# A transposed neighbour sum that transposes pairs of count bytes as 16-bit words, and back transposes placed inside the sum before it

## The reference

```python
x = _layernorm(x + _L0_gnn_ref(x, ...))   # two graph convolutions
x = _layernorm(x + _L1_gnn_ref(x, ...))   # two segment means and a GRU cell
x = _layernorm(x + _L2_gnn_ref(x, ...))   # MLP over node, summed edge features, graph
x = _layernorm(x + _L3_gnn_ref(x, ...))   # two neighbour-mean layers
```

```python
feat_in = h @ W_in.T + b_in
feat_out = h @ W_out.T + b_out
a_in = _seg_mean(feat_in[src], dst, N)     # over the edges that enter a node
a_out = _seg_mean(feat_out[dst], src, N)   # over the edges that leave a node
h = _gru_cell(jnp.concatenate((a_in, a_out), axis=1), h, ...)
```

## Time and profile before

| | us |
|---|---|
| median of 3 runs | 1025.28 |
| lowest, highest | 1022.96, 1034.95 |
| profiled execution, its time | 1021.54 |
| span of the profiled execution | 1019.8 |
| TensorE busy | 942.5 |
| VectorE busy | 622.6 |
| ScalarE busy | 483.9 |
| GpSimd busy | 60.2 |

### The profile page before, as it was taken

How to read it: one execution, slowest core, us unless ns; L and a number is a source line. 1 busy time by engine, 2 the same in 40 slices (tenths; PEclk the granted TensorE clock), 3 DMA queues, 4 the chain that set the end, 5 groups by cost and what they waited for, 6 DMA issues and landing times.

```text
span 1019.8 us, 19249 instructions
## 1 busy us (share of the span) xinstructions
PE 942.5 (92%) x7324; PEld 827.3 (81%) x7324; DVE 622.6 (61%) x949; ACT 483.9 (47%) x785; POOL 60.2 (6%) x133
## 2 busy tenths in 40 slices
PE   7599999999689999989989989989999799999995
PEld 6499999999689979989988878845444499969995
DVE  3799999899364455665554445535465655504654
ACT  0245444444565565677547757722532432233233
POOL 1200000000000000000002324400000000000000
PEclk9989999899799999989999989999999899999998
DMA  9767877777100000000000000000000000000001
GB/s 283 142 143 171 178 164 168 155 170 155 30 1 0 0 1 1 1 16 1 0 1 0 0 1 0 0 2 1 11 1 0 22 1 0 0 1 1 1 12 53
DMA packets 168790, 48.11 MB, mean 47 GB/s; under 512 B 155068, under 2 KB 167388, under 8 KB 168713
## 3 DMA queue, kind: packets, MB, share of 16 engines
q1 hardware_dynamic: 155582, 44.96, 19.0%
q10 hardware_dynamic: 12012, 0.83, 0.8%
q0 software_dynamic: 1120, 1.29, 0.5%
HBM read 45.44 MB, written 8.02 MB: 52 GB/s over the span
## 4 chain that ended last, share of the span: by engine, by line
PE 85%; DVE 5%; SPq 3%; ACT 3%; DMA 2%; issue 2%; DVEq 0%; ACTq 0%
PE bank L1638 17%; PE bank L1639 17%; PE bank L1581 10%; PE bank L1571 7%; PE bank L1757 5%; PE bank L1750 4%; PE bank L1758 4%; PE bank L1842 2%; PE bank L1792 2%; PE bank L1543 2%; PE bank L1831 1%; PE bank L1793 1%; PE bank L1686 1%; PE bank L1850 1%; PE bank L1830 1%
## 5 line engine op out<-in xcount | busy, mean ns | idle before, releaser
L1638 PE MATMUL bank<-stage,f_hi 125*128 125x392 f32 x1000 | 347.8, 348 | 8.9 <-DVE f_lo L1096 2.8
L1639 PE MATMUL bank<-stage,f_lo 125*128 125x392 f32 x1000 | 343.5, 343 | 0.0
L1075 DVE CAST stage<-counts 125x2352 fp32r<-125x2352 uint8 (+1 forms) x120 | 165.4, 1380 | 87.4 <-PE bank L1639 87.3
L1638 PEld LDWEIGHTS bank<-stage,f_hi 125*128 125x128 f32 x1000 | 190.7, 191 | 11.4 <-issue 5.6
L1639 PEld LDWEIGHTS bank<-stage,f_lo 125*128 125x128 f32 x1000 | 190.5, 190 | 0.6
L740 ACT ACTIVATE stage<-counts 125x1568 fp32r<-125x1568 uint8 (+1 forms) x80 | 107.8, 1347 | 173.4 <-PE bank L1639 170.7
L1581 PE MATMUL bank<-tmp,wb 128*65 128x25 f32 x2000 | 133.6, 221 | 0.9 <-DMA wb<-in_edge_attr 0.6
L1581 PEld LDWEIGHTS bank<-tmp,wb 128*65 128x65 f32 x2000 | 130.5, 145 | 1.3 <-DMA wb<-in_edge_attr 0.7
L686 ACT ACTIVATE counts<-bank 125x500 uint8<-125x500 f32 x188 | 87.9, 537 | 46.1 <-PE bank L1571 45.2
L844 ACT ACTIVATE stage<-bank 125x500 fp32r<-125x500 bf16 x150 | 87.5, 588 | 36.7 <-PE bank L1750 26.7
L1571 PE MATMUL bank<-rowb,xT 128*128 128x125 bf16 x1250 | 89.8, 229 | 8.4 <-DVE rowb L1007 3.8
(11 more groups left out here) (215 smaller groups left out, 944.9 us busy)
## 6 DMA issues: line engine op xcount, KB each, us to landing
wb<-in_edge_attr SPq DMA_DIRECT2D x125, 256.0 KB, 3.6
lists_d<-in_dst SPq DMA_DIRECT2D x1, 3104.0 KB
lists_d<-in_src SPq DMA_DIRECT2D x1, 3104.0 KB
wa<-in_x SPq DMA_DIRECT2D x25, 62.5 KB
out<-wl SPq DMA_DIRECT2D x6, 250.0 KB
xT<-in_dst SPq DMA_DIRECT2D x63, 4.0 KB, 3.1
xT<-in_dst ACTq DMA_DIRECT2D x62, 4.0 KB, 2.8
wb<-in_L_gnn_w_ih SPq DMA_DIRECT2D x1, 384.0 KB, 3.1
```

What stands on the lines that cost most here:

```text
L1075: nc.vector.tensor_copy(set_buffer(u, m), counts[:, SETS[u][0]:sum(SETS[u]), chunk(pair * 2 + off)]).then_inc(s["set_d_ready"], 1)
L1638: mm(bank[h][:, 0:CH], f_hi[:, first + k, :], rhs[:, k, :], start=(first + k == 0), stop=False)
L1639: last = mm(bank[h][:, 0:CH], f_lo[:, first + k, :], rhs[:, k, :], start=False, stop=(first + k == HI - 1))
```

## The change

The transposed sum is written anew.

- A pair of neighbouring count bytes is read as one 16-bit word (FP16) without conversion. TensorE transposes 128 words x 125 source nodes at a time against a new identity `ident_h`; the result in PSUM has, on partition p, the two counts of target nodes 2p and 2p+1 of a block of 256. The copy from PSUM reads the bytes (stride 2) and writes two tiles of fp32r, one for the even and one for the odd nodes. There are 12 blocks of 128 words and a last one of 32 words, which becomes a single tile of 64 rows. 120 is the new largest count for which the dense path is taken.
- The stationary tiles have to be the features of nodes a, a+2, a+4, ...; they are made anew, in seven sets, by transposing strided columns of `xT` on TensorE (bank 3), with an upper part by ScalarE and a rest by VectorE. `f_cur` and GpSimd's copies are gone.
- Step u transposes the words of step u+1 (eight tiles, then the remaining four or five), and multiplies two tiles per group. ScalarE copies the first eight transposed tiles, VectorE the others. There are no hardware loops.
- Factor rows are spread in the even steps of the first half, and copied by ScalarE; VectorE marks edges in the odd steps, and makes `has_edges` in two parts in the second half. The sums are kept bank by bank, and the waits of the second half and of the gates are by bank.
- The first norm's back transposes are issued inside the third sum, group c-1 in chunk c, ahead of its fourth set; the third sum is unrolled on TensorE and ScalarE.
- `n_small` moves to free columns of `wl1`.

The diff, cut to its core:

```diff
-        f_hi = sb("f_hi", [LO, HI, D], F32R)
-        f_lo = sb("f_lo", [LO, HI, D], F32R)
-        stage = sb("stage", [LO, 2 * NP], F32R)
+        f_hi_all = sb("f_hi", [D, HI, D], F32R)
+        f_lo_all = sb("f_lo", [D, HI, D], F32R)
+        stage_all = sb("stage", [D, 4 * TQ], F32R)
+        ident_h = sb("ident_h", [128, 128], FP16)
...
+        words = counts[:, :, :].bitcast(FP16)
+        def t_words(u, hi):
+            a = u % TT * TW
+            if u % TT < TT - 1:
+                return [(slice(0, TW), words[:, hi, a:a + TW])]
+            return [(slice(0, NP // 2 - a), words[:, hi, a:NP // 2])]
+        def t_pair(u, p):
+            return (THALF[u // TT][0] + 8 * p, (8, 4 + u // TT)[p])
+        def t_bank(u, p):
+            return bank[4 + 2 * (u % 2) + p]
...
# ScalarE
-            rest_of_sum(2, ((0, 0, 1), (0, 0, 3)))
-            for k in (0, 2, 4, 6):
-                keep_back(0, k)
+            for c in range(NC):
+                if c:
+                    widen_set(2, c // 2, c % 2, 1)
+                    widen_set(2, c // 2, c % 2, 3)
+                if c % 2:
+                    keep_back(0, c - 1)
+            def bytes_to_rows(u):
+                act.wait_ge(s["tile_t"], 2 * u + 1)
+                for to, of in t_copies(u, 0):
+                    last = nc.scalar.activation(to, of, ACT.Copy)
+                last.then_inc(s["tile_ev_a"], 1)
+            def source_tiles(j):
+                act.wait_ge(s["f_t"], j + 1)
+                for rows, tiles, made in f_parts(j):
+                    last = nc.scalar.activation(f_hi_all[rows, tiles, :], made, ACT.Copy)
+                last.then_inc(s["f_split"], 1)
+            bytes_to_rows(0)
+            source_tiles(0)
+            for u in range(2 * TT - 1):
+                if u < TT:
+                    if u % 2:
+                        source_tiles(u // 2 + 1)
+                    else:
+                        g, n = GROUPS[u // 2]
+                        act.wait_ge(s["row_made"], NGR + u // 2 + 1)
+                        nc.scalar.activation(wb[:, g * LO:(g + n) * LO], bank[3][:, 0:n * LO], ACT.Copy).then_inc(s["row_kept"], 1)
+                bytes_to_rows(u + 1)
...
# VectorE
+            def keep_sums(half):
+                for k in ((0, 1, 2), (3, 4, 5, 6))[half]:
+                    g, n = GROUPS[k]
+                    dve.wait_ge(s["rows_used"], k + 1)
+                    dve.wait_ge(s["edges_marked"], 2 * k + 2)
+                    nc.vector.tensor_tensor(wb[:, g * LO:(g + n) * LO], bank[k % 3 if k < 6 else 3][:, 0:n * LO], wb[:, g * LO:(g + n) * LO], ALU.mult).then_inc(s["tsum_kept"], 1)
+            bytes_to_rows(0)
+            source_tiles(0)
+            for u in range(2 * TT - 1):
+                if u < TT and u % 2:
+                    source_tiles(u // 2 + 1)
+                bytes_to_rows(u + 1)
+                if u == TT - 1:
+                    keep_sums(0)
+                if u % 2 and u // 2 < NGR:
+                    mark_edges(u // 2)
...
+            keep_sums(1)
...
# TensorE
-            neighbour_sum(2)
-            for k in range(NGR):
-                back_group(0, k)
+            def back_in_sum(c):
+                if c:
+                    if c - 1 < 4:
+                        wait_scaled(pe, 0, c + 1)
+                    back_group(0, c - 1)
+            for c in range(NC):
+                sum_chunk(2, c // 2, c % 2, back_in_sum)
+            def transpose_pair(u, p):
+                hi, n = t_pair(u, p)
+                for h in range(n):
+                    for rows, of in t_words(u, hi + h):
+                        last = nc.tensor.transpose(t_bank(u, p)[:, :].bitcast(FP16)[rows, h * 126:h * 126 + LO], of, ident_h[:LO, :LO])
+                last.then_inc(s["tile_t"], 1)
+            def sum_group(u, g):
+                n = t_group(u // TT, g)[1]
+                w = n * LO + n % 2
+                pe.wait_ge(s["tile_ev_a" if g < 2 else "tile_ev_d"], u + 1)
+                if u == TT:
+                    if g < 3:
+                        pe.wait_ge(s["tsum_kept"], g + 1)
+                    else:
+                        pe.wait_ge(s["row_kept"], 2 * NGR)
+                rows = t_rows(u)
+                for q, kt in t_pieces(u):
+                    o = (u % 2 * 2 + q) * TQ + g * 4 * LO
+                    rhs = stage_all[:rows, o:o + w]
+                    mm(bank[g][:, 0:w], f_hi_all[:rows, kt, :], rhs, start=(kt == 0), stop=False)
+                    last = mm(bank[g][:, 0:w], f_lo_all[:rows, kt, :], rhs, start=False, stop=(kt == 2 * TT - 2))
+                if u % TT == TT - 1:
+                    last.then_inc(s["rows_used"], 1)
+            for p in range(2):
+                transpose_pair(0, p)
+            wait_back_all(pe, 0)
+            source_tiles(0)
+            for u in range(2 * TT):
+                if u < TT:
+                    if u % 2:
+                        pe.wait_ge(s["row_kept"], NGR + u // 2 + 1)
+                        source_tiles(u // 2 + 1)
+                    else:
+                        if u == 0:
+                            pe.wait_ge(s["out_ready"], 1)
+                        pe.wait_ge(s["f_rest"], u // 2 + 1)
+                        g, n = GROUPS[u // 2]
+                        spread(bank[3], out_inv[:, g:g + n], n).then_inc(s["row_made"], 1)
+                for g in range(t_groups(u)):
+                    if u + 1 < 2 * TT and g < 2:
+                        transpose_pair(u + 1, g)
+                    sum_group(u, g)
```

More of the change, by code:

```diff
@@ L281, in gnn_program, with f_rows, f_columns @@
+        def f_rows(kt):
+            return t_rows(kt // 2)
+        def f_columns(kt):
+            a = 2 * TW * (kt // 2)
+            if kt < 2 * TT - 2:
+                return [xT[:, a + kt % 2:a + kt % 2 + 2 * TW - 1:2]]
+            return [xT[:, a + q:NP:2] for q in range(2)]
         GROUPS = [(g, min(4, HI - g)) for g in range(0, HI, 4)]
@@ L1753, in sum_group @@
-            def sum_group(half, par, g, first, final):
-                n = t_group(half, g)[1]
-                w = n * LO + n % 2
-                rhs = stage[:, t_row(par, g):t_row(par, g) + w]
-                mm(bank[g][:, 0:w], f_cur[:, par, 0, :], rhs, start=first, stop=False)
-                return mm(bank[g][:, 0:w], f_cur[:, par, 1, :], rhs, start=False, stop=final)
-            def step(half, j, par, first=False, final=False):
-                pe.wait_ge(s["f_cur_made"], j + (HI * half + 1))
-                for g in range(THALF[half][1]):
-                    pe.wait_ge(s["tile_ev_d" if g == 3 else "tile_ev_a"], t_evac_count(half, j, g))
-                    if not final:
-                        transpose_group(half, j + 1, 1 - par, g)
-                    last = sum_group(half, par, g, first, final)
-                last.then_inc(s["rows_used"], 1)
@@ L1771, in _ @@
-            for half in range(2):
-                if half:
-                    pe.wait_ge(s["tsum_kept"], 1)
-                for g in range(THALF[half][1]):
-                    transpose_group(half, 0, 0, g)
-                step(half, 0, 0, first=True)
-                step(half, 1, 1)
-                with pe.Fori(1, HI // 2) as t:
-                    step(half, t * 2, 0)
-                    step(half, t * 2 + 1, 1)
-                step(half, HI - 1, 0, final=True)
-                pe.wait_ge(s["out_ready"], 1)
-                for g in range(THALF[half][1]):
-                    hi, n = t_group(half, g)
-                    spread(out_row[g], out_inv[:, hi:hi + n], n).then_inc(s["row_made"], 1)
@@ new lines, in source_tiles @@
+            def source_tiles(j):
+                columns = [of for kt in F_SETS[j] for of in f_columns(kt)]
+                for i, of in enumerate(columns):
+                    last = nc.tensor.transpose(bank[3][:f_rows(F_SETS[j][0]) // (1 if len(F_SETS[j]) > 1 else 2), i * D:(i + 1) * D], of, ident[:, :])
+                last.then_inc(s["f_t"], 1)
+            def sum_group(u, g):
[15 more added lines that the diff above has]
+                    last.then_inc(s["rows_used"], 1)
```

222 lines of the change are left out of this document (94 added, 128 removed).

## The result

The changed kernel runs in **990.29 us** (median of 4, 987.47 to 994.18), the kernel before in 1024.12 in the same rounds (median of 4, 1022.39 to 1034.95). The ratio is 0.967, with a 95% interval of 0.963 to 0.972. The profiled execution took 987.47 us with a span of 985.4, against 1021.54 and 1019.8. The forecasts were 986.6 for it and 989 for the median; both come out within 1.3 us, and inside the range of 980 to 1005.

The account below looks back on a forecast made before the run. TensorE's stream was taken as the bound. Transposed sum 107.2 against 143.7 us (36.5 less), gates 1.5 less, third sum 3.1 more: net 34.9 off 1021.54, so 986.6, median 989; range 980 to 1005.

Parts of the forecast that it names:

- the boundary: Pause between the halves of the transposed sum: banks come free one by one, so 9.1 us becomes 0.8.
- the third sum: Back transposes moved into it, where TensorE has no pause: 3.1 us longer, their copies costing nothing.
- The steps and pauses: Transposed sum: steps 99.6, first pause 6.6, half boundary 0.8, end 0.2, together 107.2 us against 143.7.
- Factor rows: Broadcasts moved from the pauses into the transposed sum's steps, 0.118 us each; with source tiles 5.1 us.
- First pause and low clock: Ahead of the transposed sum's first product: 5.1 us plus 1.5 for the lower clock behind it, 6.6 against 9.3.
- Count transposes: In the steps: 313 at 0.06 us by load width plus 50 returns to products at 0.04, 20.8 us.
- The gates: Behind the transposed sum: they start at once, 7.2 us becomes 0.2, and low clock mostly goes, 1.5 us less.
- the sum of 27.6: Count transposes in the steps if the fast weight load does not apply: 27.6 us in place of 20.8.
- Eviction: Copies from PSUM in the steps: ScalarE 1.85 us, VectorE 1.20 and 1.46; under the step, so they cost nothing.
- Rival 1: Count transposes: the load is not faster for 16-bit words, +6.8 us, 996; chance 0.11.
- Rivals 2 to 4: Half-rate PSUM byte reads, 999 (0.11); one-step look-ahead too short, 1004 (0.12 with Rival 5); eviction the bound, 1057 (0.06).
- Rival 5: Steps keep their waits for row factors or sources; sized like the look-ahead rival, 1004, sharing its chance of 0.12.

Follow-up runs that it names:

- e4: The changed kernel with every count transpose issued twice, same output: 1014.28 us, ratio 0.990 to the kernel before.
- e7: The changed kernel with step 0's source tiles put ahead of its count transposes and byte copies on all three engines: 994.04 us, ratio 0.966 to before.
- e8: The changed kernel with both edits, factor rows spread by transposes and source tiles first: 988.84 us, ratio 0.964 to before.
- e3: The changed kernel with blocks of 124 words in place of 128, last 85 target nodes left out: 991.58 us, ratio 0.969 to before.
- e9: The changed kernel with the second half's first product waiting until all three banks of the first half are kept: 994.29 us, ratio 0.970 to before.
- e10: The changed kernel with the same count transposes in three runs a step (4, 4, 4 or 5) in place of two: 995.68 us, ratio 0.970.
- e1: The changed kernel with the first norm's back transposes put back behind the third sum: 994.34 us, ratio 0.972 to before.
- e12: The same kernel as e8, run again in the same rounds as the unedited changed kernel: 986.66 us, ratio 0.960 to before.
- e5: The changed kernel with each ScalarE byte copy made twice, first into scratch: 999.57 us, ratio 0.973 to before.
- e11: The changed kernel run once more, unedited, for a second profile: 992.26 us, six runs.
- e6: The changed kernel with each factor broadcast made a transpose, one instruction instead of two, also ahead of the first sum: 994.43 us, ratio 0.971.

## Why the prediction was right, and where it was not

**Which resource.** Right: the steps are TensorE's stream (e4), with no wait in either half. The pauses went as the prediction says: 0.71 us of idleness at the boundary (forecast 0.8), gates 0.20 us behind the last product (0.2), the third sum 2.84 longer (3.1), GpSimd idle. Which engine sets the pace and what the pauses cost is thus the forecast's own mechanism.

**Size.** The steps and pauses were to be 107.2 us and are 109.5; the net of the stages was to be 34.9 and is 31.1.

- *Factor rows.* The prediction took the earlier trace rows, `x24` in 2.84 us, as 24 broadcasts of 0.118. The x counts instructions, and a 4-byte product with the identity is two, so it was twelve broadcasts of 0.237. The 21 in the steps were booked at 2.5 us and cost about twice that: +2.4 (e7 to e8, 2.43 us). This is the term that was mis-sized.
- *First pause and low clock.* The pause takes 5.76 us against 5.1. e3 has the same 2.49 us of idleness, the same eight instructions and a clock of 1.00, and takes 5.24; so 0.52 of it is the clock, and the broadcasts' 0.44 too much are mostly made up by a chain of copies 0.3 shorter than its sum. The low clock was booked at 1.5 and costs 1.7 over the stage, pause and steps together (109.48 against e3's 107.76).
- *Count transposes* take 0.5 back (20.3 against 20.8, below). The broadcasts in the steps give +2.4, the pause at full clock +0.1 (5.24 against 5.1), the clock +0.2, and these -0.5: 2.2 of the 2.3 us.
- *The gates.* The forecast gain of 1.5 is there at their start (clock 1.00, and the first chunk takes 5.65 us where it took 7.24), and it is gone at the end: rest is 347.8 in both. The timeline of after shows where, at a wait for ScalarE that both kernels have:

```profile
692.64 0.67 PE L1733 MATMUL bank<-ident,wa 128*125 128x128 f32 x4 [1.67 <-ACT wb L818]
...
693.91 1.52 PE L1852 MATMUL bank<-wa,wl 128*128 128x392 f32 x2
```

```profile
728.67 0.67 PE L1686 MATMUL bank<-ident,wa 128*125 128x128 f32 x4 [1.66 <-ACT wb L781]
...
729.61 0.83 PE L1792 MATMUL bank<-wa,wl 128*128 128x392 f32 x2
```

The first of these is after, the second before. Behind 1.67 us of idleness two gate products take 1.52 us after, and behind 1.66 us they take 0.83 before. The granted clock was 0.83 in after's 687.6 to 697.6, and 1.00 in the same place of before and of e3:

```profile
722.00:732.00 10.00, 8.34 (x31) 4.37 (x30) 4.82 (x11) 6.92 (x14) 0.00 (x0) 1.00 0.00 0
```

```profile
693.40:703.40 10.00, 8.33 (x31) 4.37 (x30) 3.76 (x8) 5.88 (x15) 0.00 (x0) 1.00 0.00 1
```

Followed product by product, the gates of after are 1.60 us ahead of before's until this wait and 0.09 behind them right after it: the fall costs 1.7 us. A second place lies 126 us behind the first gate product, at products that wait 3.01 us for VectorE in every kernel. Its window in after and then in e8:

```profile
763.60:771.60 8.00, 6.79 (x20) 3.97 (x20) 4.66 (x14) 1.71 (x4) 0.00 (x0) 0.79 0.00 0
```

```profile
766.80:774.80 8.00, 4.94 (x20) 3.19 (x20) 6.37 (x22) 1.88 (x4) 0.00 (x0) 0.98 0.01 2
```

Before has 0.79 there as well; where it is near 1.00 (e3, e8, e9), about 1.6 us more are saved. So rest is 347.8 or 347.9 with the low clock in both places, 346.1 with the second alone (e10), and 344.6 with neither. e1 has 0.79 at the second place too, but no low clock behind its next wait, and comes to 344.9. e8 and e12, one kernel, are at 344.6 and 347.9. The gain of 1.5 at the start of the gates was sized right; what failed is that it was booked to the end of the program, with a clock taken to stay as it was. What decides a fall was not found.

**Right for another reason.** The count transposes were priced at 0.06 by their load's width, plus 0.04 a return: 20.8 us. e3, e4 and e10 give 0.052 by the 125 columns that stream, and 0.08 a return: 313 x 0.052 + 50 x 0.08 = 20.3 us. The kernel before fits the same prices: a run of four cost 0.28 us in the earlier trace rows, and 4 x 0.052 + 0.08 = 0.29. So the halving came from half as many transposes and under a third as many returns (50 for 175), and a faster load had no part in it. That the sum came out near the measured one is luck: two wrong prices made up for each other. The Trainium skill (TensorE: Matmul & The Clock Gate, section Weight-path perf modes) says the fast load is on at 128 weights of a type other than FP32. The load records agree (98 ns at 128 columns, 137 at 124), and the sum of 27.6 that I gave for the case without it is refuted: e3 is that case.

**Eviction.** Both copies came as worked out: 2000 elements 1838 ns (1.85), 1000 and 1250 elements 1200 and 1462 ns (1.20 and 1.46). These are the lines of both, after:

```profile
L883 ACT ACTIVATE stage<-bank x28: 995/1838/1845, 528.8 to 633.1; 128x2000 fp32r<-128x2000 uint8 x24, 32x1000 fp32r<-32x1000 uint8 x4
...
L1359 DVE CAST stage<-bank x28: 667/1200/1462, 529.9 to 634.4; 128x1000 fp32r<-128x1000 uint8 x12, 128x1250 fp32r<-128x1250 uint8 x12, 32x500 fp32r<-32x500 uint8 x2, 32x625 fp32r<-32x625 uint8 x2
```

(1462 - 1200) / 250 = 1.05 ns an element for one-byte reads; the earlier trace rows gave 1.03 from a two-byte and a four-byte copy. The Trainium skill (VectorE: DVE Perf Modes, section Why PSUM operands drop a tier) caps an operand in PSUM at 2×_1P, and at 1× for FP32. The trace agrees in that no faster mode appears; whether the cap or the stride of 2 keeps bytes at this rate no run here shows.

**The rivals.** Rival 1 named the wrong mechanism: a slower load costs nothing (e3). Rivals 2 to 4 needed a longer copy or a shorter look-ahead than there is: the copy could double at no cost to the steps (e5). Rival 5 fails on the windows, 71.00 us of 71.00 without a pause, and on the timeline, where TensorE waits once between its first and its last product.

**The median.** The profiled execution came to 986.6 + 0.9, but 3.3 us of its gain lie ahead of the third sum, in the scatter of the front. By the stages alone it would have been 1021.54 - 31.1 = 990.4, 3.8 above the forecast: 2.5 in the transposed sum (36.5 forecast, 34.0 measured), 1.5 in the gates, 0.26 the other way in the third sum. The error is in the terms above, and that one profile hid it was luck. 990.4 is still well inside the range.

## What to carry to other kernels

Count instructions, not operations: the count beside a row of TensorE is of instructions, and a 4-byte product with the identity is two where a 4-byte transpose is one (0.237 against 0.112 us for 125 columns). On a stream of TensorE price a small product by the columns it streams plus each change back to large products, not by the record of its load, and then double the product or the load to see which of them the pace follows. Compare kernels by stages cut at fixed instructions when an unchanged part scatters by more than the effect (10.8 us here). Compare only stretches at the same granted clock (e4's price of a transpose is 0.048 us against a kernel at low clock, 0.053 against one at full), and follow a gain in the clock to the end of the program before booking it.

## What the runs showed of the hardware that was not expected

- A FP16 transpose with 125 moving columns keeps a pace of 0.052 us whether its load's record is 98 or 137 ns (e3), and every one counts (e4, 0.053 us each against e3).
- A change from such transposes back to 500-column products costs 0.08 us on the second product (0.31 against 0.23 us), and lengthens the step by as much (e10).
- Pauses of like length did not always bring the same clock. Behind 2.48 us of idleness the 9 us from the end of the third sum had 0.81 in after, e11, e6, e9 and e10, and behind 2.49 us 1.00 in e3, whose code differs; e4, with 2.27 us, had 1.00; behind 1.28 us it was 1.00 in e7, e8 and e12. In the gates 1.67 us brought 0.83 or 1.00 in the same kernel (e12 and e8).
- A one-byte read of every second byte out of PSUM costs ScalarE 0.84 ns and VectorE 1.05 ns an element: no more than the 0.84 of the earlier trace rows (two-byte reads from PSUM, one-byte from SBUF) and the 1.03 of the earlier trace rows (two- and four-byte reads from PSUM).
